# Starting a kernel's cross attention within the last three bodies of its decoder

## What is computed

```python
x = _layernorm(x + _L0_attn_ref(x, ...))            # decoder: 4 layers, 16 heads, causal with ALiBi, FFN of 1024, final norm
x = _layernorm(x + _L0_xattn_ref(x, ctx_768, ...))  # cross attention over 120 context rows, then relu FFN of 512
x = _layernorm(x + _L0_ffn_ref(x, ...))             # 8 experts of 1024, top 2 by a router
```

## Time and profile before

| | us |
|---|---|
| median of three runs | 3541.78 |
| profiled execution | 3547.18 |
| its span, first to last instruction | 3545.4 |
| decoder: ends about | 1861.8 |
| cross attention: ends about | 2250.4 |
| TensorE busy | 3327.9 (94%) |
| VectorE busy | 2603.5 (73%) |
| ScalarE busy | 2353.1 (66%) |
| GpSimd busy | 1419.8 (40%) |

### The profile page before, as it was taken

How to read it: one execution, slowest core, us unless ns; L and a number is a source line. 1 busy time by engine, 2 the same in 40 slices (tenths; PEclk the granted TensorE clock), 3 DMA queues, 4 the chain that set the end, 5 groups by cost and what they waited for, 6 DMA issues and landing times. The chain is left out here.

```text
span 3545.4 us, 90224 instructions
## 1 busy us (share of the span) xinstructions
PE 3327.9 (94%) x36704; PEld 2322.9 (66%) x36704; DVE 2603.5 (73%) x5236; ACT 2353.1 (66%) x3538; POOL 1419.8 (40%) x1308
## 2 busy tenths in 40 slices
PE   5899999999999999999994988799999999999998
PEld 3677676776767767677762655466666666666665
DVE  4666667666676766767646888898888888888867
ACT  4677777777777777777743676566666666666665
POOL 1233232332323233232324552564454444444475
PEclk8999999999999999999996899899999999999999
DMA  3100111101111011110002122100000000000001
GB/s 121 42 29 29 41 50 37 38 29 41 42 44 36 31 41 41 45 35 31 30 1 86 57 64 75 63 13 26 1 26 26 1 26 1 26 1 26 1 13 37
DMA packets 102764, 124.56 MB, mean 35 GB/s; under 512 B 17648, under 2 KB 90608, under 8 KB 100080
## 3 DMA queue, kind: packets, MB, share of 16 engines
q1 hardware_dynamic: 102352, 118.78, 10.2%
HBM read 50.13 MB, written 8.39 MB: 17 GB/s over the span
## 5 line engine op out<-in xcount | busy, mean ns | idle before, releaser
L2708 POOL TENSOR_TENSOR e_hT<-e_h,e_hT 128x512 f16<-128x512 f32 x512 | 614.1, 1201 | 603.6 <-ACT e_hT L2457 580.6
L1017 DVE TENSOR_REDUCE mx<-maxima_pair 128x4 f16<-128x1024 f32 (+1 forms) x384 | 470.1, 1224 | 234.7 <-PE maxima_pair L504 232.2
L2451 ACT ACTIVATE e_h<-e_h,e_b 128x512 f32<-128x512 f32 x512 | 365.3, 714 | 417.4 <-DVE e_h L2537 417.3
L93 PE MATMUL bank<-xT,w_half 128*128 128x512 f16 x2304 | 535.2, 383 | 3.9 <-DVE xT L960 3.9
L815 ACT ACTIVATE PR<-scores_pair 128x1024 f32<-128x1024 f32 x384 | 392.6, 1022 | 127.5 <-PE scores_pair L521 119.0
L1123 POOL TENSOR_TENSOR QK<-qk,QK 128x512 f16<-128x512 f32 x128 | 148.2, 1158 | 629.4 <-ACT qk L744 434.2
L2395 PE MATMUL bank<-VS,e_hT 128*128 128x256 f16 x3072 | 389.5, 273 | 5.2 <-DVE VS L2500 4.1
L2395 PE MATMUL bank<-e_w,e_hT 128*128 128x256 f16 x3072 | 388.7, 273 | 4.6 <-POOL e_hT L2708 4.3
L93 PEld LDWEIGHTS bank<-xT,w_half 128*128 128x128 f16 x2304 | 216.4, 98 | 246.1 <-issue 12.5
L2395 PEld LDWEIGHTS bank<-VS,e_hT 128*128 128x128 f16 x3072 | 300.7, 98 | 112.1 <-DVE VS L2500 4.6
L2395 PEld LDWEIGHTS bank<-e_w,e_hT 128*128 128x128 f16 x3072 | 300.6, 98 | 109.9 <-POOL e_hT L2708 6.5
(11 more groups left out here) (221 smaller groups left out, 7011.1 us busy)
## 6 DMA issues: line engine op xcount, KB each, us to landing
QS<-QK SPq DMA_DIRECT2D x240, 128.0 KB, 2.1
KS<-QK SPq DMA_DIRECT2D x192, 128.0 KB, 2.1
PR<-in_expert_weights SPq DMA_DIRECT2D x16, 1024.0 KB, 4.9
stage<-in_weights SPq DMA_DIRECT2D x48, 256.0 KB, 3.5
c_x<-in_x SPq DMA_DIRECT2D x8, 512.0 KB, 4.4
xT_f<-c_xT SPq DMA_DIRECT2D x8, 512.0 KB, 3.7
stage<-xT_f SPq DMA_DIRECT2D x4, 1024.0 KB, 5.5
out<-stage SPq DMA_DIRECT2D x8, 512.0 KB, 3.5
```

Source lines behind the costliest of these rows:

```text
L93: last = pe.matmul(out, stat(a, k), mov(b, k), start=(k == 0 and n == 0), stop=(k == tiles - 1 and n == 2))
L1017: dve.tensor_reduce(out, src, AX.X, ALU.max, negate=True).then_inc(mx_in.sem, 1)
L2451: act.activation(h32[r % 2][:, j, :], h32[r % 2][:, j, :], ACT.Gelu, bias=b1[:, e, m:m + 1], scale=1.0 / WS)\
L2708: pool.tensor_tensor(hT[r % 2][1][:, f, part], h32[r % 2][:, j, :], hT[r % 2][0][:, f, part], ALU.subtract)\
```

## The change

The set-up of the cross attention moves out of its block into a class `CrossStart`, whose parts are called at the ends of LAST, TAIL and END. Scratch for it is found by sharing: both stages now use the same `w_half`, `z`, `xT32` and `xT`; the decoder's buffers of raw weights (`stage`) and of hidden rows (`spare`) take the cross attention's weights in three pieces of 1536, 1024 and 1040 columns.

- SyncE. At the end of LAST: constants, context, x0 of group 0, weights piece 0. Of TAIL: key rows, weights piece 1. Of END: x0 of group 1, weights piece 2.
- ScalarE. High half of piece 0 at the end of LAST, of piece 1 at the end of TAIL, of piece 2 in body 0 of the cross attention.
- VectorE. LAST, ahead of its `hidden_low`: a memset, stats, root and scale of group 0, stats of group 1. TAIL, ahead of its `hidden_low`: `sum_stats(0)`, the root, `sum_scaled(0)`; behind it: `first_scaled(1)`, query bias, low half of piece 0. END: stats of group 2 between the second and the third `shrunk`, low half of piece 1 at the very end. Low half of piece 2 in body 0 of the cross attention.
- GpSimd. Three `add_first` of group 0 behind the `hidden_low` of LAST, three of group 1 behind that of TAIL.
- The cross attention's bodies leave out what is done, and TensorE waits for pieces 0 and 1 at the start and for piece 2 ahead of its first `outputs`.

The diff, cut to its core (the class's functions are those of the kernel before, moved):

```diff
+class CrossStart:
+    SPLITS = ((0, 3 * KD * D), (3 * KD * D, 3 * KD * D + KD * F2), (3 * KD * D + KD * F2, 3 * KD * D + 2 * KD * F2 + KD * E))
...
+        self.w_raw = [stage[:, 0:3 * KD * D], spare[:, 4 * GT:4 * GT + KD * F2], spare[:, 0:KD * F2 + KD * E]]
...
+        self.x0 = shared["xT32"][0].rearrange("p k n -> p (k n)").rearrange("p (t d) -> p t d", t=TT)
...
+    def load_constants(self, sp):
+        sp.dma_start(self.rows[:, :], self.dram["cross_rows"].partition_broadcast(P)).then_inc(self.s_const, 16)
+        sp.dma_start(self.cols[:, :], self.dram["cross_cols"]).then_inc(self.s_const, 16)
+        sp.dma_start(self.ctx32[:, :, :], self.dram["ctx"][:, :, 0:GB * S]).then_inc(self.ctx_in.sem, 16)
...
+    def load_weights(self, sp, i):
+        if i > 0:
+            sp.wait_ge(self.s_w_in, 16 * i)
+        sp.dma_start(self.w_raw[i], self.dram["cross_weights"][:, slice(*self.SPLITS[i])]).then_inc(self.s_w_in, 16)
...
@@ decoder, block.sync @@
+            if kind is LAST:
+                start.load_constants(sp)
+                sp.wait_ge(xl1.sem, xl1.after(END_OF))
+                start.load_x0(sp, 0)
+                sp.wait_ge(w_lo.sem, w_lo.after(L - 1))
+                start.load_weights(sp, 0)
+            if kind is TAIL:
+                sp.wait_ge(M_ps.sem, M_ps.after(END_OF))
+                sp.wait_ge(S_ps.sem, S_ps.after(END_OF))
+                start.load_key_rows(sp)
+                sp.wait_ge(xb1.sem, xb1.after(END_OF))
+                sp.wait_ge(xb2.sem, xb2.after(END_OF))
+                sp.wait_ge(v_in.sem, v_in.after(END_OF))
+                start.load_weights(sp, 1)
+            if kind is END:
+                sp.wait_ge(start.mix.sem, start.mix.after(0))
+                start.load_x0(sp, 1)
+                for s in h_l:
+                    sp.wait_ge(s.sem, s.after(END_OF))
+                start.load_weights(sp, 2)
@@ decoder, block.scalar @@
+            if kind is LAST:
+                act.wait_ge(V_ps.sem, V_ps.after(END_OF))
+                act.wait_ge(QK_ps.sem, QK_ps.after(END_OF))
+                start.weights_high(act, 0)
+            if kind is TAIL:
+                act.wait_ge(OP_ps.sem, OP_ps.after(END_OF))
+                act.wait_ge(H_ps.sem, H_ps.after(END_OF))
+                start.weights_high(act, 1)
@@ decoder, block.vector @@
             if tail:
                 shrunk(kind, n, group(g, -2), 1)
+            if kind is END:
+                start.first_stats(dve, 2)
+            if tail:
                 shrunk(kind, n, group(g, -2), 2)
...
+            if kind is LAST:
+                dve.memset(start.stats[:, :, :], 1.0).then_inc(start.s_zeros, 1)
+                dve.wait_ge(start.s_zeros, 1)
+                start.first_stats(dve, 0)
+                start.joint_root(dve, 0)
+                dve.wait_ge(T1_ps.sem, T1_ps.after(END_OF))
+                start.first_scaled(dve, 0)
+                start.first_stats(dve, 1)
+            if kind is TAIL:
+                start.sum_stats(dve, 0)
+                start.joint_root(dve, 1)
+                dve.wait_ge(T2_ps.sem, T2_ps.after(END_OF))
+                start.sum_scaled(dve, 0)
             if back:
                 for m in range(KF // 2, KF):
                     hidden_low(n, m)
+            if kind is TAIL:
+                start.first_scaled(dve, 1)
+                start.query_bias(dve)
+                start.weights_low(dve, 0)
+            if kind is END:
+                start.weights_low(dve, 1)
@@ decoder, block.gpsimd @@
+            if kind is LAST:
+                pool.wait_ge(start.s_const, 16 * 2)
+                for i in range(3):
+                    start.add_first(pool, 0, i)
+            if kind is TAIL:
+                for i in range(3):
+                    start.add_first(pool, 1, i)
@@ cross, block.tensor @@
         pe.wait_ge(s_const, 16 * 3)
-        pe.wait_ge(s_w_hi, 1)
-        pe.wait_ge(s_w_lo, 1)
+        pe.wait_ge(s_w_hi, 2)
+        pe.wait_ge(s_w_lo, 2)
...
+            if n == 0 and k == 0:
+                pe.wait_ge(s_w_hi, 3)
+                pe.wait_ge(s_w_lo, 3)
@@ cross, block.scalar @@
-        act.wait_ge(s_w_in, 16)
-        act.activation(w_half[0][:, :], w_raw[:, :], ACT.Copy, scale=WS).then_inc(s_w_hi, 1)
...
+            if n == 0:
+                start.outputs_high(act)
@@ cross, block.vector @@
-            if has(n + 2):
-                first_scaled(n + 2)
+            if has(n + 2) and n + 2 > 1:
+                start.first_scaled(dve, n + 2)
...
             if has(n + 1):
                 maxima(n + 1, 0, 0)
+            if n == 0:
+                start.outputs_low(dve)
```

More of the change, by code:

```diff
@@ L1107, in _ @@
     def _(pool):
-        for s in (v_in, qk_l, h_l[0], xb1, xb2):
+        for s in (v_in, qk_l, h_l[0], xb1, xb2, start.mix):
             pool.sem_inc(s.sem, s.credit())
@@ L1179, in cross @@
     xT_f32 = dram["xT_f32"]
[L1181 to L1195, removed]
-    ctx = [[sb(f"c_ctx{i}_{h}", [P, KD, GB * S], F16) for h in range(2)] for i in range(2)]
[L1197 to L1207, removed]
+    start = shared["start"]
+    rows, cols, qbias, x0, ctx32 = start.rows, start.cols, start.qbias, start.x0, start.ctx32
+    row, router_bias = start.row, start.router_bias
+    views = start.views
+    ctx = [[sb(f"c_ctx{i}_{h}", [P, KD, GB * S], F16) for h in range(2)] for i in range(2)]
+    z, xT = shared["z"], shared["xT"]
+    xT32 = shared["xT32"][1]
     h32 = sb("c_h32", [P, KF2, GT], F32)
-    hT = [sb(f"c_hT{h}", [P, KF2, GT], F16) for h in range(2)]
+    hT = [w[:, 2 * KF2 * GT:3 * KF2 * GT].rearrange("p (m n) -> p m n", m=KF2) for w in shared["w_half"]]
     logit = sb("c_logit", [P, TT, E], F32)
@@ L1218, in sig @@
         return Signal(sem("c_" + name), per, unit)
[L1220 to L1224, removed]
+    s_const, s_w_in, s_w_hi, s_w_lo, s_qb = start.s_const, start.s_w_in, start.s_w_hi, start.s_w_lo, start.s_qb
+    x0_in, ctx_in = start.x0_in, start.ctx_in
+    zf, mix, z1, z1b = start.zf, start.mix, start.z1, sig("z1b", 1)
     T1_ps, xh1, xl1 = sig("T1_ps", KD), sig("xh1", KD), sig("xl1", KD)
@@ L1800, in _ @@
     def _(dve):
-        for s in (*stats_in, rooted, zf, z1, xl1, mx_in, rd_in, on_in, ol, y_in, z2, xl2, route):
+        for s in (xl1, mx_in, rd_in, on_in, ol, y_in, z2, xl2, route):
             dve.sem_inc(s.sem, s.credit())
         dve.wait_ge(s_const, 16 * 3)
[L1805 to L1814, removed]
@@ L1847, in scale_tiles @@
-        def scale_tiles(i, n, src, out, done):
-            rstd = root[NEWTON % 2]
-            dve.wait_ge(rooted.sem, rooted.after(n))
-            for t in range(TT):
-                at = i * TT + t
-                dve.tensor_scalar(out(t), src(t), mean_var[:, at, 0:1], rstd[:, at:at + 1], ALU.subtract, ALU.mult)\
-                   .then_inc(done.sem, 1)
-        def first_stats(n):
-            tile_stats(0, x_tiles(n))
-        def first_scaled(n):
-            dve.wait_ge(z1.sem, z1.after(n - 1))
-            scale_tiles(0, n, x_tiles(n), lambda t: z[0][:, t:t + 1, :], zf)
-            if n == 0:
-                split_weights()
@@ L1999, in _ @@
                 first_weights_sum(5)
-            if has(n + 3):
-                first_stats(n + 3)
+            if has(n + 3) and n + 3 > 2:
+                start.first_stats(dve, n + 3)
             if has(n):
@@ L2031, in _ @@
                 last_stats(n - 2)
-            if has(n + 2):
-                sum_stats(n + 2)
+            if has(n + 2) and n + 2 > 0:
+                start.sum_stats(dve, n + 2)
             if has(n):
                 maxima(n, 3, 1)
-            if 0 <= n + 3 < NG + LAG:
-                joint_root(n + 3)
+            if 1 < n + 3 < NG + start.LAG:
+                start.joint_root(dve, n + 3)
             if has(n - 2):
                 last_scaled(n - 2)
-            if has(n + 2):
+            if has(n + 2) and n + 2 > 0:
                 sum_scaled(n + 2)
@@ L2114, in _ @@
         for n in BODIES:
-            if has(n):
-                add_first(n, 0)
+            if has(n) and n > 1:
+                start.add_first(pool, n, 0)
             if has(n - 2):
@@ L2119, in _ @@
                 values(n - 2, 1)
-            if has(n):
-                add_first(n, 1)
-                add_first(n, 2)
+            if has(n) and n > 1:
+                start.add_first(pool, n, 1)
+                start.add_first(pool, n, 2)
             if n == NG + 2:
```

191 lines of the change are left out of this document (129 added, 62 removed).

## The result

The changed kernel takes 3519.22 us, the median of six runs, against 3540.32 us for six runs of the kernel before: a ratio of 0.9946 with a 95% interval of 0.9931 to 0.9961. Timed once more, five runs against nine, it was 3516.91 against 3537.26 us, 0.9936 (0.9923 to 0.9948). That is 19 to 23 us faster, a little over the half per cent that a measurement can tell.

What follows compares the result with a forecast made beforehand. The prediction took TensorE as the bound, idle at the handover to the cross attention. 27.6 + 2.7 - 1.1 - 5.0 - 0.9 - 1.2 = 22.1 us off the median 3541.78 gave 3519.7 us, range from 3507 to 2 us above 3527.

Steps and rivals of the forecast that it cites:

- The hole: TensorE's idle 30.75 us at the handover from decoder to cross attention: first turn 27.6 us earlier.
- The fill: From the cross attention's first turn to its first `maxima`: 1.9 to 3.6 us gained, 2.7 taken.
- Piece 2: Low half of the third weights piece in body 0: VectorE's 1040 added columns delay TensorE, 1.1 us lost.
- LAST: VectorE's four `hidden_low` take turns with GpSimd's three `add_first`, delaying TAIL's `outputs`: 5.0 us lost.
- two such neighbours: VectorE's `hidden_low` and GpSimd's `add_first` in LAST, two SBUF inputs each: whole-instruction turns, 3.0 us for both.
- TAIL: The root takes turns with GpSimd's `hidden_low`, so VectorE's `hidden_low` ends later: 0.9 us lost (0 to 2.0).
- The clock: A 5 us stop in TAIL puts TensorE at its lower clock level once: 1.2 us lost (0 to 1.8).
- the signs that the prediction named: Hole 3 to 4 us, `maxima` within 2.5 us, `hidden_low` rows near 3 us, turns of `On` near 1824.
- The first rival: The cover holds: LAST, TAIL and the clock cost nothing, 29.2 us gained, 3512.6; chance 0.27.
- The second: Every collision at its price, the fill gives nothing back: 14.8 us gained, 3527.0; chance 0.16.
- The last two: TensorE waits again at the boundary, 3537, chance 0.05; lower clock through most of the cross attention, 3563, chance 0.04.

Runs made afterwards that it cites:

- e1: The changed kernel with GpSimd in LAST held until VectorE's four `hidden_low` are done; one timed execution, 3517.22 us.
- e3: The changed kernel with TensorE's 13 semaphore increments for the cross attention's start moved into END; one timed execution, 3508.28 us.
- e4: The changed kernel with only fetches and weight splitting early, norms and sums back in the cross attention; one timed execution, 3533.77 us.
- e2: The changed kernel with each `add_first` of group 0 cut into four short instructions; one timed execution, 3515.62 us.
- f3: The changed kernel with e1, e3, piece 1's low half before END's last `shrunk`, and `sum_scaled(1)` behind group 0's first two `maxima`; 3507.09 us, ratio 0.9913.

## Why the prediction was right

*The hole: 27.6 predicted, 26.4 measured.* e1 has no collision, so its first turn (65.1) against 91.5 is this term. The split of piece 1 took 1.22 us, not 1.1, TensorE's increments 2.1, not 1.3, and 0.58 us are left for the boundary in e3, not 0.3. That the chain fits into LAST and TAIL with every transfer in time was right.

*The fill: 2.7 predicted, 3.0 in e1.* From first turn to first `maxima`: 18.1 before, 15.1 in e1. In the changed kernel it is 14.45; the first turns ran at the higher clock there (1.06 us against 1.94).

*Piece 2: 1.1 predicted, 0.1 to 0.3 measured.* The row of 1.76 us is there, but the first `maxima` and the experts are 340.5 us apart before and 340.6 in e1, 340.8 in the changed kernel. The `maxima` behind the row does come 1.1 us late: it follows the one ahead of the row by 2.75 us instead of 1.63. Two `maxima` further on the distance from the one ahead of the row is 8.61 us instead of 8.55: VectorE's waits for scores there are shorter (0 and 0.43 us instead of 0.39 and 0.65), and they take up most of the delay. So the price was right and the path wrong: "VectorE is what TensorE waits for there" held for one wait. No run takes piece 2 out alone, and 0.1 to 0.3 us is less than this stretch varies between the kernels (339.4 us in e3 and e4).

*LAST: 5.0 predicted, 4.0 measured.* The mechanism is as described and e1 and e2 show it. Three turns were lost, as predicted, but by the first three instructions; I had the first slip in and the last one wait. A turn took 2.6 to 2.8 us from start to start, not 3.0, and the four ended 4.85 us later behind LAST's last `shrunk` than before, not 5.4. Of that 0.81 us cost nothing, because `outputs` had waited so long for TensorE, as VectorE's timeline of the kernel before shows:

```profile
1816.19 0.26 DVE L968 RECIPROCAL rden<-bank 128x16 f32<-128x16 f32 x1 [0.81 <-PE bank L556]
```

By the Trainium skill ("SBUF — State Buffer", "Who interferes with whom") VectorE with two SBUF inputs and a GpSimd instruction that reads SBUF exclude each other, while VectorE with at most one SBUF input, outside its two-port modes, does not contend. The traces agree with the first: 8.76, 4.42 and 3.9 us for the four. With the second agree the divisions (0.42 us each) and the stats (1.39 us beside GpSimd, 1.41 alone). But the prediction took the price of "two such neighbours", with two inputs each, from `c_var`, which reads one tensor. The reading was wrong and did no harm here: VectorE's TENSOR_SCALAR with one tensor input was held too (`c_var` 2.00 us, the scales 4.08 instead of 1.38). Which mode these ran in, no view shows.

*TAIL: 0.9 predicted, 0.0 measured.* The root did take turns with GpSimd (1.02 us at 1843.37), but e1, with the same work in TAIL, has its `hidden_low` done at 48.3 as before: the four follow without a gap in 2.62 us (the changed kernel's row at 1850.36) and catch up with ScalarE, which supplies the last one no earlier.

*The clock: 1.2 predicted, 0.0 net.* Behind the new stop TensorE's rows run at the lower level (the turns 1.97 us at a granted clock of 0.50, where e1 has 1.09; the product 3.55 where e1 has 2.78): 1.6 us, the rise from 4.0 to 5.6 between the table's first two lines. But the decoder's last product, behind its 2.24 us stop, took 12.31 us before and 10.64 here, with a granted clock of 0.51 in its first 3 us before and 1.00 here. All four profiles with the stop in LAST have 10.64; of the others six have 12.31 and f3 has 10.64, so the stop may favour it and is not needed for it. That part is not settled.

*The sum.* 26.4 + 3.0 - 0.1 is e1's 29.3 us, less 3.4 net for the collision in LAST and what follows from it: 25.9 against 22.1 predicted. Each cost beside the hole was set too high, by 4.7 us together (8.2 against 3.5), and the hole 1.2 us too large; so that the forecast met the timed median within 0.5 us is in part luck. It is nearer by the timed runs (19 to 23) than by the trace. Of the signs that the prediction named, the rows of `hidden_low` came near 3 us, the turns of `On` came at 1821.35 instead of near 1824 (4.0 us later than before, counted from LAST's last `shrunk`), `maxima` 2.05 us behind the first `row_scores`, and the hole is 4.32 us, a little over the 3 to 4. From the first `row_scores` to the experts' first product it is 342.8 us instead of 345.1. The first rival, a cover that holds, is wrong about the kernel as it stands, and e1 and e2 make it true with one edit. The second had the collisions right and their prices too high, and its fill that gives nothing back is wrong (3.0 us). The last two did not come: the cross attention's clock was not lower throughout (0.73 in its first 40 us from the first turn, 0.63 before), and nothing was waited for again at the start.

## What to carry to other kernels

When work is moved beside other work, ask not only whether the engine is free but how long one instruction of its neighbour is: VectorE and GpSimd took turns by whole instructions here, and cutting GpSimd's into four, or placing them beside VectorE's reads of PSUM, took away all of the stop that the overlap had cost TensorE. Count a moved stage's small costs as well: thirteen semaphore increments were half of the hole that was left. And where other stretches vary by several us, count from marks on both sides of the stretch that was changed.

## What the runs showed of the hardware

- GpSimd's `tensor_tensor` on 1024 float32 columns and VectorE's with two SBUF inputs exclude each other per instruction: four of VectorE took 8.76 us beside three of 2.35 to 2.7 us, 4.42 beside quarters of them, and 3.9 in e1, where they only wait for ScalarE. VectorE's TENSOR_SCALAR with one tensor input was held as well: four of 256 columns took 4.08 us beside GpSimd's `hidden_low` and 1.38 with GpSimd idle. VectorE's divisions with PSUM as an input were not slowed by a running `add_first` (0.42 us each in e1, the same as before).
- A semaphore increment cost TensorE 0.16 us (13 of them 2.14 us, e3).
- The granted clock of TensorE in one stretch of ten us in the cross attention was 0.55 in one kernel and 1.00 in another that arrived there 7 us sooner, in two profiles of each. A group took 36.2 us there with the one and 32.5 with the other.
- Behind the same stop of 2.24 us the decoder's last product of 96 matmuls took 12.31 us in six profiles and 10.64 in five, the same both times in each kernel that was profiled twice. No run here explains which.
